# Adding up the weighted expert outputs on VectorE instead of GpSimd, with a new order of work, in a two-layer cross-attention and mixture-of-experts kernel

## What is computed

```python
# layer 0: attention with 16 heads over 154 context rows, then 8 experts, two of them active per row
weights = softmax(where(logits >= second_largest, logits, -inf))
h = gelu(einsum('td,edh->eth', xf, W1) + b1)          # 8 experts, 512 hidden each
expert_out = einsum('eth,ehd->etd', h, W2) + b2
out = einsum('etd,te->td', expert_out, weights)       # the weighted sum of this change
# layer 1: causal attention, cross-attention and a feed-forward, each with a layer norm,
# then 32 routed experts of 64 hidden each (6 active) and a shared one
```

## Time and profile before

| | |
|---|---|
| median of 3 runs | 594.84 us (593.46 to 596.15) |
| the profiled execution: its time | 594.72 us |
| its span, first to last instruction | 592.9 us |
| TensorE busy | 566.6 us (96%) |
| VectorE, ScalarE, GpSimd busy | 399.4, 323.7, 104.6 us |
| mean granted TensorE clock | 0.994 |

### The profile page before, as it was taken

How to read it: one execution, slowest core, us unless ns; L and a number is a source line. 1 busy time by engine, 2 the same in 40 slices (tenths; PEclk the granted TensorE clock), 3 DMA queues, 4 the chain that set the end, 5 groups by cost and what they waited for, 6 DMA issues and landing times.

```text
span 592.9 us, 8098 instructions
## 1 busy us (share of the span) xinstructions
PE 566.6 (96%) x2512; PEld 372.9 (63%) x2512; DVE 399.4 (67%) x1265; ACT 323.7 (55%) x566; POOL 104.6 (18%) x120
## 2 busy tenths in 40 slices
PE   2799999999999999999999999999899999999997
PEld 2666667665666666656676567565667766676664
DVE  4889899783212444648557675778889899677564
ACT  1478687867445466844775458854385342343221
POOL 3102020000211210242122315235200011100000
PEclk9899999999999999999999999999899999999999
DMA  2601000030211120111101021053211332342441
GB/s 78 233 19 28 1 10 2 2 143 19 58 49 36 38 71 19 35 38 36 36 35 36 2 64 36 20 175 112 89 72 53 112 109 87 113 141 67 134 138 40
DMA packets 23306, 38.35 MB, mean 65 GB/s; under 512 B 3776, under 2 KB 9536, under 8 KB 22880
## 3 DMA queue, kind: packets, MB, share of 16 engines
q1 hardware_dynamic: 22832, 37.44, 19.9%
q10 hardware_dynamic: 432, 0.40, 0.3%
HBM read 36.45 MB, written 1.38 MB: 64 GB/s over the span
## 4 chain that ended last, share of the span: by engine, by line
PE 84%; DVE 7%; ACT 4%; issue 3%; DMA 1%; POOL 1%; ACTq 0%; DVEq 0%
PE ps L1682 17%; PE ps L1493 10%; PE ps L1495 9%; PE ps L1494 9%; PE ps L1852 9%; PE ps L1569 4%; PE ps L1488 4%; PE ps L1589 3%; PE ps L1500 2%; PE ps L1604 2%; PE ps L1601 2%; PE ps L1759 2%; PE ps L1739 1%; PE ps L1749 1%; DVE NM L1156 1%
## 5 line engine op out<-in xcount | busy, mean ns | idle before, releaser
L1493 PE MATMUL ps<-xThi,w1s 128*128 128x512 f32 x256 | 144.4, 564 | 2.1 <-DVE h L1445 2.1
L911 ACT ACTIVATE h<-ps,early 128x512 f32<-128x512 f32 x128 | 86.8, 687 | 79.5 <-PE ps L1495 65.7
L1682 PE MATMUL ps<-h,w2s 128*128 128x512 f32 x256 | 122.1, 594 | 0.2 <-DVE ty L1245 0.2
L1495 PE MATMUL ps<-xTlo,w1s 128*128 128x512 f32 x256 | 101.4, 396 | 0.0
L1494 PE MATMUL ps<-xThi,w1s 128*128 128x512 f32 x256 | 100.8, 394 | 0.0
L1002 ACT ACTIVATE s<-ps 128x512 f32<-128x512 f32 x68 | 40.7, 599 | 101.2 <-PE ps L1495 100.9
L1493 PEld LDWEIGHTS ps<-xThi,w1s 128*128 128x128 f32 x256 | 48.6, 190 | 36.5 <-issue 16.9
L1682 PEld LDWEIGHTS ps<-h,w2s 128*128 128x128 f32 x256 | 46.7, 189 | 33.4 <-issue 24.1
L1445 DVE TENSOR_TENSOR h<-s,ps 128x512 f32<-128x512 f32 x68 | 46.5, 684 | 28.7 <-PE ps L1495 25.8
L1494 PEld LDWEIGHTS ps<-xThi,w1s 128*128 128x128 f32 x256 | 48.8, 190 | 25.9 <-issue 21.4
L1852 PE MATMUL ps<-h,w2s 128*128 128x512 f32 x128 | 64.2, 594 | 0.9 <-DVE h L1451 0.9
(11 more groups left out here) (264 smaller groups left out, 884.8 us busy)
## 6 DMA issues: line engine op xcount, KB each, us to landing
CB<-ct_rows SPq DMA_DIRECT2D x128, 128.0 KB, 2.9
WB<-wt_rows SPq DMA_DIRECT2D x32, 256.0 KB, 3.2
w2s<-w_dram SPq DMA_DIRECT2D x2, 2048.0 KB, 8.1
raw<-gu_dram SPq DMA_DIRECT2D x4, 512.0 KB, 5.5
x_in<-x_dram SPq DMA_DIRECT2D x4, 256.0 KB, 2.8
w2s<-dn_dram SPq DMA_DIRECT2D x1, 1024.0 KB, 7.2
out_dram<-ty SPq DMA_DIRECT2D x4, 256.0 KB, 2.9
late<-late_dram SPq DMA_DIRECT2D x1, 608.5 KB, 7.5
```

The source lines that it names most:

```text
L911: nc.scalar.activation(h32[:, c % HR, :], bank[c % 2], ACT.Gelu, bias=b1T[:, c:c + 1]).then_inc(b_gelu.sem, 1)
L1493: M(dst, w[0], xThi[:, x, :], start=start, stop=False)
L1495: return M(dst, w[0], xTlo[:, x, :], start=False, stop=stop)
L1682: M(bank[2], w2s[:, c * P:(c + 1) * P], h32[:, c % HR, :], start=(c % 4 == 0), stop=(c % 4 == 3)).then_inc(b_y.sem, 1)
```

## The change

The sum of the weighted expert outputs moves from GpSimd to VectorE, as an instruction of its own behind the multiplication. The order tables of all engines were searched anew with the same rule, so nearly every number in them differs. Two waits come with the new order: SyncE's load of the next context now waits for the keys' product too, and the values' product on TensorE waits for the context itself, since it now comes ahead of the keys' product. Instruction counts are otherwise the same.

```diff
@@ SyncE, load_context
             yield
+            sp.wait_ge(a_k_ps.sem, a_k_ps.at(b, 0))
             sp.wait_ge(a_v_ps.sem, a_v_ps.at(b, 0))
@@ GpSimd
-        def stage_b(b):
-            for e in range(E0):
-                yield
-                pool.wait_ge(b_ty.sem, b_ty.at(b, e + 1))
-                if e:
-                    pool.wait_ge(b_acc.sem, b_acc.at(b, e))
-                else:
-                    pool.wait_ge(b_base.sem, b_base.at(b, 1))
-                nc.gpsimd.tensor_tensor(acc_o[:], acc_o[:], ty[:, e % 2, :], ALU.add).then_inc(b_acc.sem, 1)
@@ VectorE, stage_b
                 V.tensor_tensor(ty[:, e % 2, :], bank[2], WB[:, e % 2, :], ALU.mult).then_inc(b_ty.sem, 1)
+                yield
+                dve.wait_ge(b_ty.sem, b_ty.at(b, e + 1))
+                if e:
+                    dve.wait_ge(b_acc.sem, b_acc.at(b, e))
+                else:
+                    dve.wait_ge(b_base.sem, b_base.at(b, 1))
+                V.tensor_tensor(acc_o[:], acc_o[:], ty[:, e % 2, :], ALU.add).then_inc(b_acc.sem, 1)
@@ TensorE, context_values
             yield
+            pe.wait_ge(a_ctx_in.sem, a_ctx_in.at(b, 32))
             claim(5)
@@ PLAN_POOL
-    "split1": [[35289, 35847, 39343, 40314, 41383]],
+    "split1": [[19341, 36543, 36783, 40201, 41628]],
```

More of the change, by code:

```diff
@@ L107 @@
 PLAN_SP = {
[L108 to L116, removed]
@@ L122 @@
+    "spread_second": [[38091, 38359, 38371, 38389, 38401, 40499, 40634, 40892, 41206, 41531, 41687, 42036, 42389,
[4 rows of a table added]
 }
 PLAN_POOL = {
[L124 to L131, removed]
@@ L132 @@
-    "split1": [[35289, 35847, 39343, 40314, 41383]],
[L133 to L136, removed]
+    "constants": [[0, 15, 32, 60, 289, 340, 697]],
+    "norm_a": [[569, 596], [1627, 1654], [3576, 3603], [7079, 7107]],
@@ L137 @@
+    "norm_d": [[28530, 28557], [34870, 34897], [43115, 43142], [50211, 50238]],
 }
@@ L180 @@
+    "prepare_d": [[34340, 35748, 38028], [40805, 42044, 44855], [46048, 46398, 49265], [51381, 51602, 53394]],
+    "stage_d": [[39813, 40116, 40300, 40530, 40753, 40940, 41296, 41617, 41775, 42197, 42825, 43135, 43319, 43702,
[4 rows of a table added]
 }
 PLAN_DVE = {
[L182 to L184 removed]
@@ L185 @@
-    "masks": [[443, 897], [1748, 2714], [5164, 5561], [8312, 8330]],
-    "keys": [[1027, 1072, 1115, 1146, 1210], [1982, 2757, 2790, 2821, 3701], [5321, 5641, 5751, 6007, 6064], [8433,
-        8572, 8605, 8636, 8956]],
-    "values": [[1272, 1317, 1475, 2091, 2099, 2210], [4754, 5124, 5217, 5460, 5468, 5476], [7811, 7856, 8197, 8466,
-        8474, 8482], [10613, 10762, 11023, 11056, 11064, 11072]],
-    "queries": [[1412, 1484, 1546, 1560], [3493, 3565, 3628, 3641], [6224, 6707, 7211, 7224], [9066, 9508, 9747, 9761]
-        ],
@@ L249 @@
-    "stage_d": [[40184, 40388, 40639, 40715, 40811, 40888, 41110, 41227, 41499, 41565, 41637, 41747, 41819, 41910,
[8 rows of a table removed]
+    "constants": [[0, 949, 959, 1170, 1178, 1186, 1194, 1202, 18337, 18351]],
+    "normalised": [[441, 531, 704, 722, 741, 766, 784, 836], [1499, 1589, 1990, 2009, 2113, 2166, 2211, 2303], [3447,
+        3538, 4528, 4571, 4589, 4640, 4725, 4776], [6913, 7022, 7214, 7523, 7604, 7950, 8114, 8166]],
+    "masks": [[772, 975], [2016, 2107], [4827, 4913], [7919, 8401]],
+    "keys": [[982, 1027, 1060, 1091, 1137], [1880, 2708, 2741, 2772, 2818], [5403, 5614, 5647, 5678, 5725], [7956,
+        8488, 8521, 8669, 8828]],
@@ new lines @@
+    "values": [[1425, 1470, 2396, 2404, 2412, 2420], [4538, 4833, 4905, 4919, 5324, 5332], [7533, 7797, 7835, 7926,
+        7934, 7942], [10570, 11098, 11136, 11144, 11229, 11237]],
+    "queries": [[1218, 1289, 1352, 1365], [3228, 3300, 3362, 3375], [5989, 6394, 6560, 6774], [8861, 9206, 9268, 9281]
+        ],
+    "biased": [[890], [2428], [4057], [5226]],
+    "split0": [[2928, 3768, 5552, 5758, 7048, 9757, 10603, 11039]],
+    "maxima": [[1618, 1656, 1711, 1749, 1803, 1842, 1913, 1951, 2002, 2022], [2030, 2068, 2128, 2173, 2265, 2354, 2487,
[9 rows of a table added]
@@ L258 @@
+    "stage_d": [[40023, 40185, 40436, 40490, 40562, 40700, 40821, 40950, 41134, 41331, 41459, 41544, 41615, 41844,
[8 rows of a table added]
 }
 PLAN_PE = {
-    "context_keys": [[720], [1809], [5173], [8130]],
-    "context_values": [[1150], [4565], [7619], [10533]],
-    "inputs": [[1040, 1239], [2568, 3037], [5345, 6062], [8353, 8952]],
-    "queries": [[1631, 1926, 2183, 3592], [4238, 5001, 5891, 6316], [7327, 7973, 8541, 9166], [9934, 10904, 11125,
-        12085]],
-    "keys": [[1401, 1484], [3751, 4434], [6192, 7501], [9273, 9741]],
@@ new lines @@
+    "queries": [[1437, 1825, 1989, 3397], [4034, 4766, 5656, 6080], [7093, 7642, 8095, 8959], [9563, 10640, 11191,
+        11887]],
+    "keys": [[1207, 1289], [3571, 4127], [5956, 7252], [9080, 9728]],
+    "maxima": [[1575, 1598, 1668, 1707, 1761, 1799, 1868, 1892], [1964, 2033, 2093, 2119, 2231, 2245, 2322, 2444],
[7 rows of a table added]
+    "scores": [[2050, 2177, 2208, 2291, 2340, 2421], [2625, 2796, 2819, 2946, 2983, 3102], [3350, 3487, 3510, 3614,
[5 rows of a table added]
+    "values": [[2464, 2669, 3006], [3128, 3251, 3440], [3783, 3935, 4206], [4543, 4667, 4856], [5387, 5510, 5699],
+        [6156, 6294, 6473], [6823, 6947, 7136], [7475, 7699, 7925], [8416, 8621, 8913], [9234, 9412, 9681], [9881,
+        10005, 10208], [10417, 10541, 10730], [11272, 11430, 11619], [12051, 12195, 12390], [12603, 12726, 12906],
+        [13275, 13398, 13578]],
@@ new lines @@
+    "output": [[5048, 5233], [8049, 8193], [10884, 11021], [13725, 13918]],
+    "prepare_b": [[10777, 11720, 13013], [15936, 16446, 19028], [21829, 23013, 24936], [28183, 29044, 32636]],
+    "first": [[13169, 13494, 13770, 13847, 14008, 14077, 14495, 14620, 14689, 15104, 15173, 15331, 15400, 15554, 15623,
[8 rows of a table added]
+    "weights": [[13636], [20121], [26456], [33559]],
+    "second": [[14151, 14237, 14323, 14409, 14760, 14846, 14932, 15018, 15245, 15468, 15692, 15778, 16051, 16137,
[8 rows of a table added]
+    "stage_c": [[14576, 16691, 18780, 20006, 20210, 20990], [26380, 26769, 26901, 26987], [33785, 33930, 34092, 34178]
+        , [39951, 41095, 41279, 41365]],
```

174 lines of the change are left out of this document (84 added, 90 removed), and 182 rows, old and new, of tables (PLAN_ACT, PLAN_DVE, PLAN_PE, PLAN_SP).

## The result

The changed kernel takes 588.13 us, the median of 4 runs (587.47 to 589.0), beside 595.41 us for the kernel before on the same chip: a ratio of 0.9886, with a 95% interval of 0.986 to 0.9913. The profiled execution took 588.73 us, with a span of 586.7 us.

The account below looks back on a forecast made before the run. TensorE bounds the kernel, busy 566.6 of 592.9 us, so only its idle time and low clock can be gained. From 594.72 us, -3.5 - 3.3 + 0.2 = -6.6 us gave 588, range 585.5 to 594.0.

Parts of the forecast that it names:

- The start, -3.5: Program start: mask's cast behind the norm's small steps lets the input's statistics and TensorE's transposes begin earlier, -3.5 us.
- rival 2: Start brings only 1.5 us, low clock or VectorE's queue eating the rest; stage d's block gone: 589.9 us, chance 0.10.
- Theory A: Start brings 3.5 us, last piece 3.3, sum about nothing; low clock at the start takes some back.
- B: Theory for the experiments: stage a's own chain takes back the start's gain.
- The start of stage d, -3.3: Last GpSimd piece, rounded later, no longer blocks VectorE: -1.8 us of TensorE idle and -1.5 us of low clock.
- The block of L1352: Start of stage d: VectorE's L1352 takes 2.74 us beside the last GpSimd piece, median 0.69; counted as gone.
- the third piece's 1.1 us: Near stage d's start: the third GpSimd piece's cost, part of 0.87 us and of 0.3 us, forecast to stay.
- The sum, +0.2: Stage b: moving 32 sums from GpSimd to VectorE costs about nothing, +0.2 us for short waits.
- Theory C: The sum on VectorE brings most of the gain, because GpSimd's sums had blocked VectorE.
- Rival 1: Start gains 3.5 us, but a block turns up elsewhere or last piece meets a `CB` product: 591.2 us, chance 0.25.
- Rival 3: No gain: input and mask no longer 2 us apart, or stage a takes it back; block stays: 594.7 us, chance 0.09.
- Rival 4: Two GpSimd pieces in a row hold VectorE up to 4.8 us, TensorE stalls: +6.5 us, 601 us, chance 0.06.

Follow-up runs that it names:

- the first two experiments: Kernel before with only the mask's cast later on VectorE, 590.67 us; kernel before with only the last GpSimd piece's rounding later on ScalarE, 592.08 us.
- the second execution: The changed kernel profiled once more with no edit: 587.42 us.

## Why the prediction was right

The time was: 588.0 forecast, 588.13 measured. Of its three terms one was in truth of the other sign, and the other two came out smaller than forecast when they were undone in the new order (2.7 for 3.5, 1.9 for 3.3). That the sum is so close is luck.

**The start, -3.5.** The mechanism went as written: statistics at 4.11 us, transposes at 8.84 (9.0 to 9.6 was given; I had taken the sum into `X2` as hidden, but beside it GpSimd's L424 took 0.57 us for 0.23, and this went too), scores 3.0 us earlier, 3.84 us of idle gone. What was over-sized is the worth of it. In the profiled execution only 0.9 us of lead is left at the end of stage a, since TensorE ran at 1.2 GHz until 26.3 us; this is what rival 2 had said. In the second execution 2.1 us are left. By repeated times it is 2.7 us in the new order and 3.6 in the old. Theory A holds here, with a clock at the start that varies, and B falls.

**The start of stage d, -3.3.** The block of L1352 is gone for the stated reason, and the third piece's 1.1 us, which I had left in place, went as well: L1442, L1245 and the statistics beside it take their 0.69, 0.68 and 0.87 us, and the `CB` product starts behind it. Idle fell by 3.05 us. Undoing the last piece alone costs 1.9 us, doing it alone brings 2.4. Both are below 3.3, for two reasons. Each of these edits moves only part of the idle time, 1.1 us of it (3.10 to 2.02) and 1.2 (0.05 to 1.27), where I had counted 1.8. And the dip that I priced at 1.5 us does not come each time: a stall of the same length had none behind it in one execution.

**The sum, +0.2.** This step failed. Theory C is half right: the sum does not bring most, but nearly as much as each of the others. Moving it gained 2.0 us in the old order and 2.6 in the new by the times, 1.35 and 2.19 by the table of places. VectorE's load rose by 9.0 us with the sum alone (408.4 on its page for 399.4), not 11.3; in the whole change only by 4.6. I had bounded the gain by TensorE's 1.6 us of idle in 150 to 400 us. In the old order there are 0.3 us less idle in that stretch with the sum alone, and 0.4 less from 400 to 432. In the new order the bound doesn't hold: there GpSimd's sums would cost 1.8 us from 140 to 400. The error was to read "TensorE hardly waits for GpSimd's sum" as "the sum costs it nothing": with the sum back on GpSimd, 0.9 us of the waits are for the sum itself, and at least 1.0 us is for VectorE, whose short step stood beside one. I had counted these, as 10.7 us of VectorE's time, and then valued them at nothing.

The three errors cancel: 2.7 + 1.9 + 2.6 = 7.2 us by what undoing each part costs, 0.9886 of 595 gives 6.8, and 6.6 was forecast. The sum alone, which I had at +0.2, makes up for what the other two lacked.

**Rivals.** Rival 1 did not come: the last piece met a `CB` product, but came second. Rival 3 falls with the first two experiments. Rival 4's place was there, 5.17 us in one block, and cost VectorE some 1.5 us (1.25 for 0.69, 1.08 for a step whose median is 0.17) and TensorE none, as its `first` chunks covered it.

**What stays open.** It is open why the same stall is followed by a low clock in one kernel's profile and not in another's. How large each part is to better than about 1 us stays open as well, since the clock differs between executions. Of the 19 executions of the kernel before beside which the sum alone was timed, nine with a mean clock of 0.997 took 593.05 to 593.79 us, and the five at 0.989 to 0.991 took 595.32 to 596.13. The sum's gain isn't of this kind: at a mean clock of 0.994 its three executions took 592.28 to 593.06 us, and the four of the kernel before 594.17 to 595.45.

## What to carry to other kernels

An engine that blocks another need not appear under its own name in the bound engine's waits. Before costing its removal at nothing, look in the chain of each wait for short operations that take far beyond their median, and put their excess on the path, not only in the load. Where TensorE is thinly used at the start, look at the durations of like matmuls, not at the clock column alone; here nine matmuls on zeros in the gaps brought 3.3 us, as much as the new order of the start, and nothing that could be measured in the order for which they were not placed. A gain at the start should be measured over several executions, since one profile showed 0.9 us of what the times put at 2.7. And a moved instruction can be blocked at its new place: in the old order the last sum stood for 2.59 us beside a GpSimd piece.
